# Maxima of half of the input taken from 16-bit absolute values that ScalarE makes, folded pairwise on VectorE

## The chip, the cores and the metric

The kernel runs on one core of a Trainium2 chip. The metric is the device time in microseconds (us) of one execution. The engines are called by their short names: PE (TensorE, the matrix engine), DVE (VectorE), ACT (ScalarE), POOL (GpSimd) and SP (SyncE, which here only issues DMAs).

## The reference, cut to what matters

The input u has 16 sequences of 512 tokens of width 256, in 32-bit floats. What is computed is one layer:

```
q, k, v = u Wq^T + bq, u Wk^T + bk, u Wv^T + bv       (per sequence, transposed to channels by tokens)
k       = causal_conv(k, k_kernel) + k_D * k           (by FFT in the reference)
kv      = k * v
y       = (causal_conv(kv, ssm_kernel) + D * kv) * q
x       = layernorm(u + y Wo^T + bo)
h       = relu(x W_fc^T)^2 ;  m = h W_proj^T
spikes  = 5 steps of a leaky threshold unit on m, mean of the spikes
out     = layernorm(x + spikes)
```

Nothing in the reference asks for a maximum. The kernel computes its products on PE with pairs of 16-bit floats (a high and a low part), and for that it scales each operand by a power of two, found from the operand's largest absolute value.

## The kernel before, in words

Every engine has its program written out by hand, in order, and the engines are held together by semaphores: `X.wait_ge(s, n)` holds engine X until semaphore s has reached n, `.then_inc(s, 1)` raises it when the instruction is done. There is no scheduler; on one engine the order of the text is the order of execution. `link(ins)` on DVE (semaphore `vlink`) makes the next DVE instruction wait for this one.

The span has a start-up, a first phase (projections and the two convolutions, 32 groups of 8 channels, up to some 390 us) and a second phase (output projection, layernorms, feed-forward and spikes, 16 sequences). The change lies in the start-up, which is as follows.

- SP issues the loads of the convolution kernels (`k_st`), the weights (`w_st`, `wn_st`) and then the transposed input `uT` in `NU` = 8 pieces of 1 MB (L308), each with a semaphore of its own, `ld_u[n]`. A piece is `u_st[:, :, n * UP:(n + 1) * UP]`, 128 partitions by 2 x 1024 elements; `u_st` is the tile `qy` under another shape.
- DVE takes maxima of the weights (L942, L945, into `part_max`); POOL spreads them over the partitions (`partition_all_reduce`, L582); DVE makes powers of two of them (`pow2`, L926 to L930) and releases ACT by `scales1` (a memset, L963).
- ACT then scales and splits the weights: `w_st` scaled (L427), its high part `w16[:, :, 0]` (L429, semaphore `w_hi`), the two convolution kernels scaled (L431) and their high parts (L435, `kpad_hi`). POOL makes the low parts: L585 for the weights (waits for `w_hi`, raises `w_lo`) and L588 twice for the convolution kernels (raises `kpad_lo`). ACT issues the DMA of the split weights to DRAM after `w_lo` (L438) and those of the split convolution kernels after `kpad_lo` (L443, `ksplit_out`). SP waits for these and copies the convolution kernels around in DRAM and back into SBUF as shifted windows (L316, L333), for which DVE waits at L1040.
- Meanwhile DVE takes the largest absolute value of every piece of u (L942 with the tile `u_maxima`, one reduction a piece), then of the eight results (L967, `u_maxima_done`). POOL spreads it over the partitions (L591, `u_max_done`), DVE makes the scale `d_scale` of it (L926 to L930, then a memset at L971 that raises `scale_u`).
- On `scale_u` ACT begins to turn u into its 16-bit high parts (L455), DVE follows with the low parts of six pieces (L986), POOL with those of the two pieces of `POOL_PIECES` (L608), and PE begins to project (L685).

POOL's instructions at this place stand in this order: L582 (all-reduce), L585, L588 twice, L591 (all-reduce), L608 twice.

`part(kb, ...)` cuts a tile out of one large SBUF tensor, `arena`, from the offset `at[0]` on; so most tiles carry the name `arena` in the profile.

Of the kernel before, what the change touches and what calls it, by code (L numbers as in the profile page):

```python
# [5 lines left out]
ALU = mybir.AluOpType  # L6
ACT = mybir.ActivationFunctionType
F32 = mybir.dt.float32
F16 = mybir.dt.float16
BF16 = mybir.dt.bfloat16  # L10
I32 = mybir.dt.int32
AX = mybir.AxisListType
# [4 lines left out]
DT = D // P  # L17
# [16 lines left out]
NU = 8  # L34
UP = TOK // NU
BOTH = 4
PIECES = 2
EPS = 1e-5
X1S = 2.0 ** 10
# [35 lines left out]
def build(nc, uT, u, wcat, wk_n, wv_n, bias, bo, k1, k2, kd1, kd2, woT, wfT, wpT, out):  # L75
# [11 lines left out]
    with ExitStack() as ctx:  # L87
        def sb(name, shape, dt):
            return ctx.enter_context(nc.sbuf_tensor(name, shape, dt))

        def sem(name):
            return ctx.enter_context(nc.semaphore(name))
# [7 lines left out]
        u_maxima = sb("u_maxima", [P, NU + 2], F32)  # L100
# [15 lines left out]
        KB = 256  # L116
        arena = sb("arena", [P, 628 * KB // 4], F32)
        at = [0]

        def part(kb, dt, pattern=None, **dims):  # L120

            a = arena[:, int(at[0]):int(at[0] + kb * KB)]
            at[0] += kb * KB
            if dt != F32:
                a = a.bitcast(dt)
            return a.rearrange(pattern, **dims) if pattern else a
# [28 lines left out]
        spread_max = part(0.5, F32)  # L155
        at[0] = 20 * KB
        stage_at = at[0]
        wf_st = part(8, F32, "p (t n) -> p t n", t=DT)
        wp_st = part(8, F32, "p (t n) -> p t n", t=FT)
        at[0] = stage_at  # L160
# [33 lines left out]
        ld_u = [sem(f"ld_u{n}") for n in range(NU)]  # L194
# [3 lines left out]
        u_maxima_done, u_max_done, scales1, scale_u, scales2 = (  # L198
            sem(n) for n in ("u_maxima_done", "u_max_done", "scales1", "scale_u", "scales2"))
        part_max2_done, turned2, spread2, all_max2_done, scales3 = (  # L200
            sem(n) for n in ("part_max2_done", "turned2", "spread2", "all_max2_done", "scales3"))
        sum_first, moments_first, wo_first = (sem(n) for n in ("sum_first", "moments_first", "wo_first"))
        vlink = sem("vlink")

        w_scaled, w_hi, w_lo, f_hi, f_lo = (sem(n) for n in ("w_scaled", "w_hi", "w_lo", "f_hi", "f_lo"))
        u_hi, u_lo, u_scaled, u_lo_pool = (sem(n) for n in ("u_hi", "u_lo", "u_scaled", "u_lo_pool"))
# [38 lines left out]
        u_st = qy[:, :].rearrange("p (t n) -> p t n", t=DT)  # L245
# [22 lines left out]
        def windows1_of(s, half):  # L268
            return T[:, s % 2 * 2 + half]
# [31 lines left out]
        def _(sp):  # L301
# [16 lines left out]
            def load_windows(conv, half, g):  # L318
# [4 lines left out]
                if conv == 0 and half == 0:  # L323
                    sp.wait_ge(kpad_out[g % NKP], 32 * (g // NKP + 1))
                run, c = row // PIECES, HG // PIECES
                if conv:
# [4 lines left out]
                else:  # L331
                    for n in range(PIECES):
                        sp.dma_start(windows1_of(g, half)[0:HP, n * c:(n + 1) * c].rearrange("p c a n -> p (c a n)"),  # L333
# [80 lines left out]
        def _(act):  # L414
# [5 lines left out]
            def as_pairs(dst, src):  # L420
                return dst.bitcast(F32), src.bitcast(F32)

            act.wait_ge(id_done, 2)
            nc.scalar.activation(*as_pairs(causal, step_st), ACT.Copy).then_inc(causal_done, 1)
            act.wait_ge(scales1, 1)

            nc.scalar.activation(w_st, w_st, ACT.Copy, scale=w_scale[:, cW:cW + 1]).then_inc(w_scaled, 1)  # L427
# [245 lines left out]
        def _(pe):  # L673
# [160 lines left out]
            def down_first(i):  # L834
# [6 lines left out]
                for f in range(FT):  # L841
                    pe.wait_ge(h_hi, i * FT + f + 1)
                    for t in range(DT if f < BOTH else 1):
                        for w in range(2):
# [12 lines left out]
            def down_second(part):  # L857
                for f in range(BOTH, FT) if part == 0 else range(FT):
                    for h, w in ((0, 0), (0, 1)) if part == 0 else ((1, 0),):
                        last = down_part(1, f, h, w, False, f == FT - 1 and h == 1)  # L860
                if part:
                    last.then_inc(down_done, 1)
# [52 lines left out]
        def _(dve):  # L915
            links = [0]

            def link(ins):

                links[0] += 1  # L920
                ins.then_inc(vlink, 1)
                dve.wait_ge(vlink, links[0])
# [18 lines left out]
            def max_abs(dst, src, axis=AX.XY):  # L941
                link(nc.vector.tensor_reduce(dst, src, axis, ALU.max, apply_absolute_value=True))  # L942
# [18 lines left out]
            dve.wait_ge(all_max_done, 1)  # L961
            pow2(w_scale[:, 0:3], w_unscale[:, 0:3], all_max[:, 0:3], scratch[:, 0:3])
            nc.vector.memset(part_max[:, cF:cF + 3], 0.0).then_inc(scales1, 1)  # L963
            for n in range(NU):
                dve.wait_ge(ld_u[n], 16)
                max_abs(u_maxima[:, n:n + 1], u_st[:, :, n * UP:(n + 1) * UP])
            nc.vector.tensor_reduce(u_maxima[:, NU:NU + 1], u_maxima[:, 0:NU], AX.X, ALU.max).then_inc(u_maxima_done, 1)  # L967
            dve.wait_ge(u_max_done, 1)
            pow2(d_scale[:, 0:1], d_unscale[:, 0:1], u_max[:, :], scratch[:, 0:1])

# [57 lines left out]
            def mask(conv, s, g, half):  # L1028

                if conv == 0:  # L1030
                    dve.wait_ge(t_in[s % 2 * 2 + half], 8 * PIECES * (g - s % 2) + 16 * PIECES)
                else:
# [286 lines left out]
```

## Time and profile before

| what | value |
|---|---|
| median of 3 runs | 845.57 us (838.6, 845.57, 846.23) |
| the profiled execution: time | 842.78 us |
| the profiled execution: span, first to last instruction | 841.1 us |
| outside the span in it | 1.7 us |
| mean granted TensorE clock | 0.981 of 2.4 GHz |
| busy over the span: PE, DVE, ACT, POOL | 88%, 84%, 63%, 46% |
| maxima of u on DVE (L942, tile u_maxima) | 8 reductions, 18.3 us busy |

A row of the profile names the line of the kernel, the engine, the operation and what it writes and reads; `128x2048 f32` is partitions by elements and type, `xN` a count. "Idle before" is how long the engine stood still ahead of it, and `<-` names what ended that: another engine's instruction, a DMA, or "issue", which is time in which the profile shows nothing that was waited for. `POOLq`, `ACTq` and `SPq` are the issuing sides of the engines: register work, configuration and DMA issue, which don't count as busy.

### The profile page before, as it was taken

The numbers are of one execution on the slowest core, as the hardware profiler recorded it, in microseconds if no ns is written. First come the engines' busy times: TensorE is split into PE (matmuls) and PEld (weight loads), VectorE is DVE, ScalarE is ACT, GpSimd is POOL, SyncE is SP. The second block draws the span as 40 slices with busy tenths as digits, with TensorE's granted clock in tenths as the row PEclk, the third lists the DMA queues.
The fourth block names the chain that finished last, engine by engine and source line by source line (L and its number), as shares of the span: only waits on it lengthen the run. The fifth ranks groups of instructions, "written<-read, shape, count | busy, mean of one in ns | idle before, by whom it ended". The sixth has DMA issues, their size and how long they took to land.

```text
span 841.1 us, 27057 instructions
## 1 busy us (share of the span) xinstructions
PE 740.2 (88%) x11447; PEld 540.4 (64%) x11447; DVE 710.5 (84%) x1204; ACT 530.6 (63%) x623; POOL 384.2 (46%) x302
## 2 busy tenths in 40 slices
PE   0087877999999999977999999999999999999993
PEld 0077877999999999965555555554555555555541
DVE  6898655787788778888878999999999999999896
ACT  1393656788887888775546665566655665556651
POOL 0332211222222322234457866687666866677622
PEclk9999999999999999989999999999999999999997
DMA  9995767999999997892100011101111011100001
GB/s 335 346 261 143 181 156 166 212 223 225 222 223 228 229 223 166 170 237 89 48 1 26 26 50 50 50 0 50 50 50 50 0 50 50 50 26 25 26 26 50
DMA packets 55369, 100.71 MB, mean 120 GB/s; under 512 B 5664, under 2 KB 41376, under 8 KB 53280
## 3 DMA queue, kind: packets, MB, share of 16 engines
q1 hardware_dynamic: 53952, 97.94, 45.4%
q10 hardware_dynamic: 1376, 2.23, 0.7%
q8 instruction: 25, 0.41, 0.2%
q14 instruction: 16, 0.13, 0.1%
HBM read 89.92 MB, written 27.01 MB: 139 GB/s over the span
## 4 chain that ended last, share of the span: by engine, by line
PE 43%; DVE 26%; POOL 17%; issue 9%; ACT 2%; DMA 2%; SPq 0%; POOLq 0%; DVEq 0%; ACTq 0%
PE ps L699 17%; POOL arena L632 15%; PE ps L685 14%; DVE arena L1222 8%; PE ps L832 5%; PE ps L825 4%; DVE u_maxima L942 2%; DVE arena L1170 2%; DVE arena L986 2%; DVE arena L1219 2%; DVE arena L1189 2%; DVE arena L1195 2%; PE ps L803 1%; POOL arena L639 1%; DMA arena<-in_wv_n 1%
## 5 line engine op out<-in xcount | busy, mean ns | idle before, releaser
L699 PE MATMUL ps<-arena 128*128 128x64 f16 (+3 forms) x6144 | 169.5, 181 | 18.2 <-issue 8.4
L632 POOL TENSOR_TENSOR arena<-arena 128x512 f16<-128x512 f32 x124 | 174.5, 1438 | 16.7 <-ACT arena L518 16.5
L699 PEld LDWEIGHTS ps<-arena 128*128 128x128 f16 x6144 | 166.7, 97 | 19.7 <-issue 15.5
L832 PE MATMUL ps<-arena 128*128 128x512 f16 x768 | 173.2, 379 | 3.0 <-POOL arena L632 3.0
L825 PE MATMUL ps<-arena 128*128 128x512 f16 x768 | 170.8, 379 | 2.5 <-DVE arena L1195 1.6
L685 PE MATMUL ps<-arena 128*128 128x96 f16 x3072 | 140.5, 209 | 16.8 <-issue 9.9
L596 POOL TENSOR_TENSOR arena<-arena 128x512 f16<-128x512 f32 x32 | 40.9, 1278 | 235.0 <-ACT arena L461 235.0
L685 PEld LDWEIGHTS ps<-arena 128*128 128x128 f16 x3072 | 135.5, 99 | 19.7 <-issue 12.1
L1211 DVE TENSOR_TENSOR arena<-arena 128x512 f32<-128x512 f32 x128 | 136.8, 1123 | 5.2 <-POOL arena L632 4.5
L514 ACT ACTIVATE arena<-ps,read_factor 128x512 f32<-128x512 f32 x128 | 87.9, 686 | 74.9 <-PE ps L825 57.9
L832 PEld LDWEIGHTS ps<-arena 128*128 128x128 f16 x768 | 73.9, 98 | 90.7 <-POOL arena L632 9.7
L825 PEld LDWEIGHTS ps<-arena 128*128 128x128 f16 x768 | 74.2, 98 | 88.8 <-issue 3.3
L471 ACT ACTIVATE arena<-arena 64x1792 f32<-64x1792 f32 x64 | 105.2, 1688 | 17.5 <-DVE arena L1058 17.5
L466 ACT ACTIVATE arena<-arena 64x1792 f32<-64x1792 f32 x60 | 98.7, 1688 | 2.4 <-DVE arena L1040 1.7
L518 ACT ACTIVATE arena<-arena 128x512 f16<-128x512 f32 x128 | 79.5, 624 | 32.5 <-DVE arena L1211 31.1
L1222 DVE SCALAR_TENSOR_TENSOR arena<-ps,stair_at,arena 128x512 bf16<-128x512 f32 x128 | 96.1, 751 | 4.5
L502 ACT ACTIVATE arena<-arena 128x256 f32<-128x256 f32 x126 | 65.3, 589 | 35.2 <-DVE arena L1181 34.7
L636 POOL TENSOR_TENSOR arena<-arena,eps 128x4 f32<-128x4 f32 x32 | 12.1, 377 | 143.6 <-DVE arena L1175 136.3
L1058 DVE COPY arena<-arena 32x3840 f16<-32x3840 f16 x64 | 72.0, 1162 | 1.0
L803 PE MATMUL ps<-arena 128*128 128x256 f32 x256 | 59.9, 388 | 2.9 <-ACT arena L495 2.9
L461 ACT ACTIVATE arena<-arena 128x512 f16<-128x512 f32 x32 | 20.2, 631 | 58.7 <-PE ps L699 49.9
L803 PEld LDWEIGHTS ps<-arena 128*128 128x128 f32 x256 | 49.6, 195 | 11.4 <-ACT arena L495 2.5
(114 smaller groups left out, 767.0 us busy)
## 6 DMA issues: line engine op xcount, KB each, us to landing
arena<-kpad_dram SPq DMA_DIRECT2D x192, 256.0 KB, 5.7
kpad_dram<-ksplit_dram SPq DMA_DIRECT2D x64, 256.0 KB, 5.9
qy<-in_uT SPq DMA_DIRECT2D x8, 1024.0 KB, 17.3
arena<-in_u SPq DMA_DIRECT2D x16, 512.0 KB, 4.1
out<-arena SPq DMA_DIRECT2D x16, 512.0 KB, 3.0
arena<-in_k SPq DMA_DIRECT2D x2, 512.0 KB, 5.1
ksplit_dram<-arena ACTq DMA_DIRECT2D x2, 512.0 KB, 4.1
arena<-in_wfT SPq DMA_DIRECT2D x1, 1024.0 KB, 9.2
```

The costliest lines, as they stand in the source:

```text
L466: nc.scalar.activation(*as_pairs(*shifted(windows1_of(s, half))), ACT.Copy).then_inc(c1_copied[half], 1)
L471: nc.scalar.activation(*as_pairs(*widened(windows2_of(g, half), HP)), ACT.Copy).then_inc(c2_copied, 1)
L514: nc.scalar.activation(relu_h[:, f], PH[:, f % 2], ACT.Relu, scale=read_factor[:, 4:5]).then_inc(relu_ready, 1)
L518: nc.scalar.activation(h16[:, 0, f], h_square[:, f % 4], ACT.Copy).then_inc(h_hi, 1)
L632: nc.gpsimd.tensor_tensor(h16[:, 1, f], h_square[:, f % 4], h16[:, 0, f], ALU.subtract).then_inc(h_lo, 1)
L685: last = nc.tensor.matmul(o, u16[:, x, t, tok:tok + P], wcur[:, w, t], start=(k == 0), stop=(k == 3 * DT - 1))
L699: last = nc.tensor.matmul(out[:, ch * COL + delta * B:(ch + 1) * COL], taps(c, tp)[:, delta * P:(delta + 1) * P], data[:, xp, ch * COL:ch ...
L803: last = nc.tensor.matmul(PW[:, j // 2, (j % 2) * D:(j % 2 + 1) * D], yT[:, t, j * P:(j + 1) * P], wo[:, t], start=(t == 0), stop=(t == DT ...
L825: last = nc.tensor.matmul(PH[:, f % 2], wf16[:, w, t, f * P:(f + 1) * P], x16[:, r, x, t], start=(k == 0), stop=(k == 3 * DT - 1))
L832: return nc.tensor.matmul(PD[:, t], wp16[:, w, f, t * P:(t + 1) * P], h16[:, h, f], start=first, stop=last)
L1211: nc.vector.tensor_tensor(h_square[:, f % 4], relu_h[:, f], relu_h[:, f], ALU.mult).then_inc(square_ready, 1)
L1222: ins = nc.vector.scalar_tensor_tensor(c, y, stair_at[:, n:n + 1], c, ALU.is_gt, ALU.add)
```

## The change

Four of the eight pieces of u (`CAST` = 4, the first four) get their maximum in another way. ACT turns each into 16-bit absolute values (bf16), in a new tile `u_abs` of 4 x 2048 elements; it does this ahead of its wait for `scales1`. DVE takes the larger of two pieces elementwise (`fold`), three times over 2048 elements, then over 1024 and 512, takes the maximum of the last 512 and raises it by 2^-8 of itself, since the rounding to bf16 can lower a value. The other four pieces are reduced as before. A copy puts the first result beside the other four for the last reduction.

```
@@ tiles and semaphore
+CAST = 4
+        at[0] = 32 * KB
+        u_abs = part(16, BF16, "p (n x) -> p n x", n=CAST)
+        at[0] = stage_at
+        u_cast = sem("u_cast")
@@ ACT
             act.wait_ge(id_done, 2)
             nc.scalar.activation(*as_pairs(causal, step_st), ACT.Copy).then_inc(causal_done, 1)
+            for n in range(CAST):
+                act.wait_ge(ld_u[n], 16)
+                nc.scalar.activation(u_abs[:, n].rearrange("p (t x) -> p t x", t=DT), u_st[:, :, n * UP:(n + 1) * UP],
+                                     ACT.Abs).then_inc(u_cast, 1)
             act.wait_ge(scales1, 1)
@@ DVE
             nc.vector.memset(part_max[:, cF:cF + 3], 0.0).then_inc(scales1, 1)
-            for n in range(NU):
+            def fold(dst, other):
+                link(nc.vector.tensor_tensor(dst, dst, other, ALU.max))
+
+            for n in range(0, CAST, 2):
+                dve.wait_ge(u_cast, n + 2)
+                fold(u_abs[:, n], u_abs[:, n + 1])
+            fold(u_abs[:, 0], u_abs[:, 2])
+            for size in (DT * UP // 2, DT * UP // 4):
+                fold(u_abs[:, 0, 0:size], u_abs[:, 0, size:2 * size])
+            link(nc.vector.tensor_reduce(u_maxima[:, 0:1], u_abs[:, 0, 0:DT * UP // 4], AX.X, ALU.max))
+            link(nc.vector.tensor_scalar(u_maxima[:, 0:1], u_maxima[:, 0:1], 1.0 + 2.0 ** -8, None, ALU.mult))
+            for n in range(CAST, NU):
                 dve.wait_ge(ld_u[n], 16)
                 max_abs(u_maxima[:, n:n + 1], u_st[:, :, n * UP:(n + 1) * UP])
-            nc.vector.tensor_reduce(u_maxima[:, NU:NU + 1], u_maxima[:, 0:NU], AX.X, ALU.max).then_inc(u_maxima_done, 1)
+            link(nc.vector.tensor_copy(u_maxima[:, CAST - 1:CAST], u_maxima[:, 0:1]))
+            nc.vector.tensor_reduce(u_maxima[:, NU:NU + 1], u_maxima[:, CAST - 1:NU], AX.X, ALU.max).then_inc(u_maxima_done, 1)
```

On ACT, from its first instruction to the high parts of the weights (L427 before, L436 after, is the scaling of `w_st`), before:

```order
L424 ACTIVATE arena<-arena 128x64 [waits id_done]
L427 ACTIVATE arena<-arena,w_scale 128x1536 [waits scales1]
L429 ACTIVATE arena<-arena 128x8x192 [waits w_scaled]
L431 ACTIVATE arena<-arena,w_scale 128x1024 x2
L435 ACTIVATE arena<-arena 128x2x512 [waits w_scaled] x2
```

And the same place after:

```order
L429 ACTIVATE arena<-arena 128x64 [waits id_done]
L432 ACTIVATE arena<-qy 128x2048 [waits ld_u0]
L432 ACTIVATE arena<-qy 128x2048 [waits ld_u1]
L432 ACTIVATE arena<-qy 128x2048 [waits ld_u2]
L432 ACTIVATE arena<-qy 128x2048 [waits ld_u3]
L436 ACTIVATE arena<-arena,w_scale 128x1536 [waits scales1]
L438 ACTIVATE arena<-arena 128x8x192 [waits w_scaled]
```

Four activations, each with a wait for a piece of u, now stand ahead of the scaling of the weights and of all that follows it on ACT.

On DVE, from the release of ACT to the end of the maxima, before (the eight reductions differ only in the piece that they wait for, `ld_u0` to `ld_u7`):

```order
L963 MEMSET part_max 128x3 [waits vlink]
L942 TENSOR_REDUCE u_maxima<-qy 128x1 [waits ld_u0]
...
L942 TENSOR_REDUCE u_maxima<-qy 128x1 [waits ld_u7,vlink]
L967 TENSOR_REDUCE u_maxima<-u_maxima 128x1 [waits vlink]
L926 TENSOR_SCALAR scratch<-u_max 128x1 [waits u_max_done]
```

And after:

```order
L974 TENSOR_TENSOR arena<-arena 128x2048 [waits u_cast]
L974 TENSOR_TENSOR arena<-arena 128x2048 [waits u_cast,vlink]
L974 TENSOR_TENSOR arena<-arena 128x2048 [waits vlink]
L974 TENSOR_TENSOR arena<-arena 128x1024 [waits vlink]
L974 TENSOR_TENSOR arena<-arena 128x512 [waits vlink]
L982 TENSOR_REDUCE u_maxima<-arena 128x1 [waits vlink]
L983 TENSOR_SCALAR u_maxima<-u_maxima 128x1 [waits vlink]
L951 TENSOR_REDUCE u_maxima<-qy 128x1 [waits ld_u4,vlink]
...
L987 COPY u_maxima<-u_maxima 128x1 [waits vlink]
L988 TENSOR_REDUCE u_maxima<-u_maxima 128x1 [waits vlink]
```

Four of the eight reductions are gone, seven instructions stand in their place, and the first two of these wait for ACT, not for a DMA.

On POOL the order is unchanged; before (`ISA` without a wait is what the trace names MODIFY_POOL_CONFIG at the same lines):

```order
L582 ISA all_max<-part_max 128x11 [waits part_max_done]
L585 ISA
L585 TENSOR_TENSOR arena<-arena 128x8x192 [waits w_hi]
L588 TENSOR_TENSOR arena<-arena 128x2x512 [waits kpad_hi] x2
L591 ISA
L591 ISA u_max<-u_maxima 128x1 [waits u_maxima_done]
```

Nothing moved there, and what each of the three kinds of instruction waits for is the same as before.

## Rows read from the trace of the kernel before

**Rows 1.** The chain that ended last, 36 to 43 us: start us, us, what.

```profile
34.48 2.30 DVE u_maxima L942
36.78 0.02 issue
36.80 0.17 DVE u_maxima L967
36.98 1.80 issue
38.78 0.39 POOL u_max L591
...
40.07 2.01 ACT arena L455
```

**Rows 2.** Timeline of POOL, 14 to 42 us: start us, us busy, instruction, [idle before].

```profile
16.96 0.43 POOL L582 PARTITION_ALL_REDUCE all_max<-part_max  x1 [14.31 <-DVE part_max L959]
24.60 3.09 POOL L585 TENSOR_TENSOR arena<-arena 128x1536 f16<-128x1536 f32 x1 [7.21 <-issue]
27.66 4.19 POOL L588 TENSOR_TENSOR arena<-arena 128x1024 f16<-128x1024 f32 x2
38.78 0.38 POOL L591 PARTITION_ALL_REDUCE u_max<-u_maxima  x1 [6.93 <-issue]
```

**Rows 3.** POOL's configuration instructions, by line: durations min/median/max ns, first and last start us.

```profile
L582 POOLq MODIFY_POOL_CONFIG  x2: 11/11/11, 2.6 to 2.6; - x2
L585 POOLq MODIFY_POOL_CONFIG  x2: 102/102/102, 17.3 to 17.4; - x2
L591 POOLq MODIFY_POOL_CONFIG  x2: 2/2/2, 32.0 to 32.1; - x2
L608 POOLq MODIFY_POOL_CONFIG  x2: 83/83/83, 39.1 to 39.1; - x2
```

**Rows 4.** Timeline of ACT, 2 to 60 us.

```profile
18.36 1.57 ACT L427 ACTIVATE arena<-arena,w_scale 128x1536 f32<-128x1536 f32 x1 [14.43 <-DVE part_max L963]
19.97 1.48 ACT L429 ACTIVATE arena<-arena 128x1536 f16<-128x1536 f32 x1
21.36 2.17 ACT L431 ACTIVATE arena<-arena,w_scale 128x1024 f32<-128x1024 f32 x2
23.44 1.99 ACT L435 ACTIVATE arena<-arena 128x1024 f16<-128x1024 f32 x2
27.71 0.35 ACTq L438 DMA_DIRECT2D w_dram<-arena  x1
31.88 0.91 ACTq L443 DMA_DIRECT2D ksplit_dram<-arena  x2
51.56 1.91 ACT L453 ACTIVATE arena<-qy 128x2048 f16<-128x2048 f32 x1
```

**Rows 5.** Line L308, the issues at 3.4, 5.9 and 14.0 us (pieces 0, 3, 7), one answer each.

```profile
L308 SPq DMA_DIRECT2D qy<-in_uT x1: 832/832/832, 3.4 to 3.4; - x1
DMA to landing us min/median/max: 11.2/11.2/11.2
...
L308 SPq DMA_DIRECT2D qy<-in_uT x1: 478/478/478, 5.9 to 5.9; - x1
DMA to landing us min/median/max: 16.3/16.3/16.3
...
L308 SPq DMA_DIRECT2D qy<-in_uT x1: 2439/2439/2439, 14.0 to 14.0; - x1
DMA to landing us min/median/max: 19.6/19.6/19.6
```

**Rows 6.** Timeline of all engines, 0 to 90 us: DVE's pieces of u, beside POOL and not.

```profile
42.21 4.62 DVE L986 SCALAR_TENSOR_TENSOR arena<-qy,d_scale,arena 128x2048 f16<-128x2048 f32 x2 [0.17 <-ACT arena L455]
55.52 4.29 DVE L986 SCALAR_TENSOR_TENSOR arena<-qy,d_scale,arena 128x2048 f16<-128x2048 f32 x1
59.28 4.48 POOL L608 TENSOR_TENSOR arena<-qy,arena 128x2048 f16<-128x2048 f32 x1 [1.62 <-ACT arena L453]
```

**Rows 7.** Groups by form on DVE: count, busy us, mean ns, idle before.

```profile
L942 DVE TENSOR_REDUCE u_maxima<-qy 128x1 f32<-128x2048 f32 x8 | 18.3, 2285 | 0.3
L945 DVE TENSOR_REDUCE scratch<-arena 128x2 f32<-128x512 f32 x2 | 1.4, 686 | 0.1
L942 DVE TENSOR_REDUCE part_max<-scratch 128x1 f32<-128x2 f32 x3 | 0.5, 155 | 0.1
```

**Rows 8.** Line L1040, 40 to 60 us: DVE's first 16-bit products, waiting for the windows.

```profile
L1040 DVE TENSOR_TENSOR arena<-arena x2: 410/410/411, 52.9 to 53.3; 64x512 f16<-64x512 f16 x2
```

**Rows 9.** Line L333, the issue at 42.7 us: the last half of the first windows.

```profile
L333 SPq DMA_DIRECT2D arena<-kpad_dram x1: 595/595/595, 42.7 to 42.7; - x1
DMA to landing us min/median/max: 8.3/8.3/8.3
```

## The prediction

> **What bounds the kernel now.** The change lies in the first 40 us, so I read only that stretch, and ask what sets the moment at which ACT may begin to turn u into 16-bit parts (`scale_u`, 40.07 us). Everything after it, 800 us, hangs on that moment and on the DMAs of the split convolution kernels, and the loops behind it have no tie to absolute time. A start-up that is d longer makes the kernel d longer.
>
> First view, the chain of waits [rows 1]. It walks back from ACT L455 at 40.07 through DVE's small scale steps to POOL's all-reduce L591 at 38.78, and then shows 1.80 us of "issue" before it reaches DVE's last reduction of u, whose result was there at 36.98. The chain goes on along DVE's eight reductions, and a hasty reader takes them as the bound. The 1.80 us is where to stop: DVE was done and POOL did not start.
>
> Second view, POOL's own timeline [rows 2]. POOL finished L588 at 31.85 (27.66 + 4.19) and sat idle 6.93 us until 38.78, with "issue" as its reason. The same had happened once before: L582 ended at 17.39, L585 began 7.21 us later at 24.60, though what it waits for, ACT's L429 (`w_hi`), was done at 21.45 (19.97 + 1.48) [rows 4]. The third view says what lies in both gaps: MODIFY_POOL_CONFIG runs right after the last instruction of the other kind, at 17.4 for L585 and at 32.0 for L591, when its semaphore wait has not even begun to matter [rows 3]. After a change of kind (all-reduce to elementwise and back) POOL's first instruction comes about 7 us after the configuration, whatever else is ready. At L582 and L608 the same 7 us lie in longer waits. In sentences the rest can do without: the Trainium skill, page GPSIMD Engine Reference (the part on wrapper-ucode dispatch), says that the first call into a freshly loaded kernel pays an instruction load of about 6 us; the trace agrees in kind, with 7.21 and 6.93. With 6 in place of 6.93 the two chains would still both wait for POOL, by 0.9 us instead of 1.8.
>
> So the path in this stretch is POOL's: load of code to 24.60, L585 3.09 us, L588 4.19 us, load of code 6.93 us, all-reduce at 38.78. Two other chains join it with slack: DVE's maxima (done 36.98, slack 1.80 us) and ACT's high parts of the weights (done 21.45, slack 24.60 - 21.45 = 3.15 us).
>
> **Part one: what ACT gains in work.** Four Abs activations over 128x2048, f32 in, 16 bit out. The nearest row is ACT L453, the same size and the same kind of types without a scale from a tile: 1.91 us [rows 4]. They wait for the pieces of u. Piece 0 lands at 3.4 + 11.2 = 14.6 us and piece 3 at 5.9 + 16.3 = 22.2 us [rows 5]; between pieces there are some 2.5 us, more than 1.91, so ACT keeps pace with the DMAs and the fourth Abs runs from 22.2 to about 24.15. That the copy at L424 and Abs share a table is likely, because the order of instructions after the change has one table load as before.
>
> ACT is in order. Behind these four stands `w_st`'s scaling, which began at 18.36 and now begins at about 24.2: 5.85 us later. That is the term with the price. Queued with it are `w_hi`, the convolution kernels' high parts, and ACT's two kinds of DMA issues. Who waits: POOL L585 waits for `w_hi`, which comes at 21.45 + 5.85 = 27.3 instead of 21.45. POOL is ready at 24.60, since its load of code started at 17.4 as before. It now starts at 27.35 or so: **2.75 us later**. Of the 5.85 us, 3.1 us vanish in the slack. The high parts of the convolution kernels are there in time for L588 (L435's first half ends near 24.5 + 5.85 = 30.35, POOL finishes L585 at 27.35 + 3.09 = 30.45; the second at 31.3, before 32.5). So POOL ends L588 at 34.6, configures, loads for 6.93 us, and the all-reduce starts at 41.55 rather than 38.78: + 2.77.
>
> The other branch is ACT's DMAs. The one at 27.71 goes to 30.5 and the ones at 31.88 to 34.65, both + 2.8, because they wait for POOL and not for ACT. The windows for DVE L1040 then come 2.8 us later, and so does DVE at L1040 [rows 8]. All chains are shifted alike, so no new wait arises between them.
>
> **Part two: what DVE loses and gains.** Four reductions at 2.29 us go: 9.1 us [rows 7]. In come three folds of 2048, one of 1024, one of 512, a reduction of 512 (0.69 us, the row of L945) and a scalar step and a copy at 0.16 (the row of a two-element reduction) [rows 7]. No row shows a 16-bit fold of this size. From below: L1040 takes 0.41 us for 512 16-bit elements [rows 8]; with 0.15 us of it fixed, as the two-element reduction shows, 2048 elements come to 0.15 + 4 x 0.26 = 1.2 us, 1024 to 0.67 us. From above: L986, two inputs from SBUF with 32-bit data, 2.31 us each when alone (4.62 for two) [rows 6]. I take 1.2, since L1040 is the same operation on 16-bit data. The Trainium skill, VectorE: DVE Perf Modes (the perf-mode tier table), has 1224 ns for a 16-bit two-input operation of 2048 elements and a single speed for reductions; by it the fold would cost the same as by my lower bound.
>
> But DVE cannot use this, because it waits for ACT. The first fold is hidden (pieces 0 and 1 are cast by 19.1, it runs to 20.4). The second waits for the fourth Abs, 24.15. From there: 1.2 + 1.2 + 0.67 + 0.41 + 0.69 + 0.16 and some 0.2 of gaps = 4.5, to 28.7. Four reductions at 2.32 including their gap bring it to 38.0, copy and last reduction to 38.35. Before it was 36.98. So DVE's maxima end 1.4 us **later** than before, not sooner. Even without that wait the gain would be small, since piece 7 lands only at 14.0 + 19.6 = 33.6 [rows 5]; its reduction cannot end before 35.9, and it ended at 36.78. Both are covered: POOL is not ready before 41.55, which leaves 3.2 us. With the dear folds (2.31) the maxima end near 41.4, still just covered.
>
> **The sum.** + 2.8 us from POOL's later start, nothing from DVE. Against the profiled execution: 842.78 + 2.8 = 845.6 (span 843.9). That execution lies 2.8 under the median shown; the three runs and it spread over 7.6 us. I set the prediction against the middle of all four executions, 844.2 (between 842.78 and 845.57): **847.0 us**, a loss of 0.33%. About 1% is what a measurement of this kernel can tell from no change, so this counts as no change.
>
> **Rivals.**
> 1. *POOL's gaps are not a load in the background, but a delay after the wait.* Then the 3.15 us before L585 and the 1.80 before L591 follow the release. Against it: two gaps of 7.21 and 6.93 that agree when measured from the configuration, and disagree when measured from the release [rows 1 to 4]. It would give L585 at 30.45, + 5.85; the all-reduce at 38.35 + 1.8 = 40.15, + 1.4; and the windows + 5.85. DVE reaches L1040 1.4 later (54.3) and waits for windows that come 5.85 later. L1040 had little slack (the last of its windows landed at 42.7 + 8.3 = 51.0 [rows 9]; now 56.9). Total about + 4: 848.2.
> 2. *Folds collide with POOL and DVE becomes the bound* (this one ends clearly slower than before). L986 takes 4.29 us beside POOL's L608 and 2.31 alone, while reductions take 2.29 beside POOL's L585 and L588 all the same; L608 itself took 4.48 [rows 2, 6, 7]. Two-input work on DVE collides, reductions do not. The Trainium skill, SBUF — State Buffer (the single rule), says the same. If folds are also dear (2.31 alone, 4.3 beside POOL), then from 27.35 on, when POOL works, the third fold, those of 1024 and 512 are slowed: third done at 30.2, then 2.2 and 1.2 us, and the rest ends at 34.6; four reductions 43.9, end 44.3. That is 2.7 us over 41.55, so + 5.5: 849.7. It decides from the point where folds cost over 2.3 us each. With 1.2 us folds, only the last small one meets POOL.
> 3. *Nothing or a small gain.* If the change doesn't hold ACT up, because the pieces land sooner or POOL's load is longer than I think, or if DVE's maxima are the bound after all as the chain suggests. Then the most is 0.9 us (to the landing of piece 7): 843.3 to 844.2. Against it: ACT's order and piece 3's landing at 22.2 are facts of the trace.
> 4. *Something outside this stretch*: DMA timing in the first phase that falls otherwise after a shift. No row speaks for it; either sign, a few us.
>
> **How the numbers follow.** Forecast 0.65; rival 1 0.10; rival 2 0.12; rival 3 0.08; rival 4 0.05. The range takes the spread of the runs shown with the forecast added (838.6 + 2.8 = 841.4 to 846.23 + 2.8 = 849.0), widened up to rival 2 (846.23 + 5.5 = 851.7, cut to 851) and down by one for rival 3: 840.5 to 851. All cases lie within 1% of before (8.4 us), so same 0.94, slower 0.05, faster 0.01.
>
> **What would show it in the profile after.** ACT: four rows of L432, about 1.9 us each, the last starting when piece 3 has landed (near 22.2), and L436 near 24.2. POOL: L594 (the low part of the weights) near 27.4, its idle time now ended by ACT and no longer by "issue"; the second load unchanged near 6.9 us; all-reduce near 41.6. DVE: folds at 1.2 us, a wait before the second fold, last maximum near 38.4, then some 3 us of waiting. ACT's first conversion of u near 42.8, against 40.07. I am wrong if POOL's first gap after `w_hi` stays at 3 us (rival 1), if a fold takes over 2 us or the all-reduce is released by DVE (rival 2), or if the first conversion is where it was and the time still moves.

## The result, and the profile after

The kernel after the change takes 847.19 us (median of 20 executions, 842.5 to 850.09), the kernel before 843.49 us (median of 20, 838.6 to 848.37). The ratio is 1.0042, with a 95% interval of 1.0026 to 1.0058: a loss of 2.2 to 4.9 us, under 1%. The profiled execution of the kernel after took 849.43 us (span 847.7 us).

The chain that ended last, 20 to 44 us of the kernel after (answers to [rows 1]); start us, us, what:

```profile
5.80 16.33 DMA qy<-in_uT
22.13 0.02 issue
22.15 1.92 ACT arena L432
...
24.16 1.24 DVE arena L974
25.42 1.24 DVE arena L974
26.68 0.70 DVE arena L974
27.41 3.21 DVE arena L974
30.65 0.70 DVE u_maxima L982
...
38.52 2.30 DVE u_maxima L951
...
41.03 0.17 DVE u_maxima L988
41.20 0.13 issue
41.32 0.39 POOL u_max L600
...
42.62 2.01 ACT arena L464
```

ACT's first conversion of u now starts at 42.62 us, against 40.07 [rows 1]: 2.55 later. The 1.80 us of "issue" ahead of POOL's all-reduce has shrunk to 0.13, an ordinary hand-over, and the chain goes on through DVE, the fourth Abs and piece 3's DMA. One row in it is out of line: the fold of 512 elements takes 3.21 us, where the fold of 1024 ahead of it took 0.70.

The timeline of POOL and ACT in the kernel after, 0 to 90 us (answers to [rows 2] and [rows 4]):

```profile
22.15 1.91 ACT L432 ACTIVATE arena<-qy 128x2048 bf16<-128x2048 f32 x1 [0.66 <-DMA qy<-in_uT]
23.97 1.56 ACT L436 ACTIVATE arena<-arena,w_scale 128x1536 f32<-128x1536 f32 x1
25.56 1.48 ACT L438 ACTIVATE arena<-arena 128x1536 f16<-128x1536 f32 x1
27.13 3.20 POOL L594 TENSOR_TENSOR arena<-arena 128x1536 f16<-128x1536 f32 x1 [9.85 <-ACT arena L438]
30.30 4.38 POOL L597 TENSOR_TENSOR arena<-arena 128x1024 f16<-128x1024 f32 x2
41.32 0.38 POOL L600 PARTITION_ALL_REDUCE u_max<-u_maxima  x1 [6.65 <-DVE u_maxima L988]
```

The scaling of the weights starts at 23.97 instead of 18.36, POOL's low part at 27.13 instead of 24.60, and its releaser is no longer "issue" but ACT. POOL is free at 34.68 (30.30 + 4.38), 2.83 later than before. What ends its second idle time is now put down to DVE. So two chains arrive at the all-reduce almost together, and the profile alone doesn't say which of them counts. "Load of code" is my name for what fills POOL's idle time after its configuration changes; the traces show the configuration and the wait behind it, and what POOL does in it no run shows.

### The profile page after: what moved, and what is told of

Same layout as the page of the kernel before. It is cut to its first block, busy times and chain, and to the rows that moved or that the text cites. A ratio compares the mean times of both kernels' runs of the same rounds, so it can differ in the third digit from the quotient of the medians.

```text
span 847.7 us, 27063 instructions
## 1 busy us (share of the span) xinstructions
PE 744.2 (88%) x11447; PEld 543.2 (64%) x11447; DVE 708.6 (84%) x1208; ACT 538.1 (63%) x627; POOL 385.0 (45%) x302
## 4 chain that ended last, share of the span: by engine, by line
PE 45%; DVE 24%; POOL 15%; issue 9%; DMA 4%; ACT 2%; SPq 1%; POOLq 0%; DVEq 0%; ACTq 0%
PE ps L708 17%; PE ps L694 14%; POOL arena L641 13%; DVE arena L1243 7%; PE ps L834 6%; PE ps L841 5%; DVE arena L1007 2%; DVE arena L1240 2%; DVE arena L1191 2%; DMA qy<-in_uT 2%; DVE arena L1216 2%; DMA arena<-kpad_dram 2%; DVE arena L1210 2%; PE ps L812 1%; DVE u_maxima L951 1%
## 5 line engine op out<-in xcount | busy, mean ns | idle before, releaser
L812 PE MATMUL ps<-arena 128*128 128x256 f32 x256 | 58.7, 382 | 2.9 <-ACT arena L504 2.9
L1061 DVE TENSOR_TENSOR arena<-arena 64x512 f16<-64x512 f16 (+1 forms) x128 | 45.5, 377 | 13.3 <-DMA arena<-kpad_dram 11.8
```

## The experiments

Besides the ratio I read two moments from each trace: when POOL's all-reduce of u starts, and when ACT's first conversion of u starts ("conversion" below). These come out alike to about 0.1 us in two profiles of one kernel, which the whole time does not: of the kernel before they are 38.78 and 38.69, 40.07 and 39.98, of the kernel after 41.32 twice, 42.62 and 42.61.

**Abs on ACT alone (e1).** ACT's four activations stay, DVE takes all eight maxima as before. `u_abs` is written and never read.

```
-            (folds, reduction and scaling of u_abs, 4 reductions, copy)
+            for n in range(NU):
+                dve.wait_ge(ld_u[n], 16)
+                max_abs(u_maxima[:, n:n + 1], u_st[:, :, n * UP:(n + 1) * UP])
```

> The changed kernel with its four Abs activations on ACT in place, ahead of the weights, but with DVE taking all eight maxima of u from the 32-bit pieces as before the change; the 16-bit tile is written and not read. My theory (ACT's delay of the weights makes POOL start late, and POOL's second load of code then sets the start): POOL's low part of the weights starts near 27.1 us instead of 24.6, DVE's maxima are done near 37.0, the all-reduce of u starts near 41.3 us all the same, idle time before it put down to issue, and the time is 1.003 of before. Rival (DVE's longer chain sets the start): with DVE's chain back at 37.0 the all-reduce starts at about 38.8 and the time is that of before.

Measured: 1.003 (1.0007 to 1.0052), 846.76 us. The timeline of this kernel:

```profile
27.03 3.10 POOL L594 TENSOR_TENSOR arena<-arena 128x1536 f16<-128x1536 f32 x1 [9.85 <-ACT arena L438]
30.10 4.21 POOL L597 TENSOR_TENSOR arena<-arena 128x1024 f16<-128x1024 f32 x2
36.59 0.16 DVE L976 TENSOR_REDUCE u_maxima<-u_maxima 128x1 f32<-128x8 f32 x1
40.59 0.38 POOL L600 PARTITION_ALL_REDUCE u_max<-u_maxima  x1 [6.29 <-issue]
41.88 7.68 ACT L464 ACTIVATE arena<-qy,d_scale 128x2048 f16<-128x2048 f32 x4 [10.97 <-DVE cell L980]
```

DVE is done at 36.75 and the all-reduce starts at 40.59 all the same. So the activations on ACT alone, with DVE as it was, make the conversion 1.8 us late (41.88 against 40.07) and the kernel slower. The rival, 38.8, is out. But it came 0.7 us short of my 41.3: the second load of code lasted 6.29 us here, not 6.93, and in the kernel after the all-reduce starts 0.73 later than this.

**The folds alone (e2).** No Abs on ACT; POOL fills `u_abs` with zeros at the very start, so that the maximum leaves out the first four pieces of u.

```
-            for n in range(CAST): (wait for ld_u[n], Abs on ACT)
+            nc.gpsimd.memset(u_abs.rearrange("p n x -> p (n x)").bitcast(F32), 0.0).then_inc(u_cast, CAST)
```

> DVE does the changed kernel's folds and its four remaining reductions, but ACT has no Abs: the 16-bit tile is filled with zeros by POOL at the very start, so the maximum leaves out the first four pieces of u. My theory: ACT's weights are back at 18.4 us and POOL at 24.6; DVE's folds all run before POOL works and take 1.22, 1.22, 1.22, 0.69 and 0.4 us, its maxima are done about 36.3 (piece 7 lands at 33.6), the all-reduce starts near 38.8 as before, held by POOL's load of code, and the time is that of before (1.000, within 0.002). Rival (DVE's chain sets the start): 0.7 us sooner than before. Second rival (folds themselves cost something elsewhere): slower than before with ACT and POOL unmoved.

Measured: 1.0011 (0.9989 to 1.0034), 844.02 us. DVE's maxima are done at 34.97, sooner than I reckoned (36.3), and the all-reduce waits for 3 us more:

```profile
24.68 3.08 POOL L591 TENSOR_TENSOR arena<-arena 128x1536 f16<-128x1536 f32 x1 [7.76 <-issue]
27.74 4.20 POOL L594 TENSOR_TENSOR arena<-arena 128x1024 f16<-128x1024 f32 x2
34.81 0.16 DVE L985 TENSOR_REDUCE u_maxima<-u_maxima 128x1 f32<-128x5 f32 x1
38.00 0.38 POOL L597 PARTITION_ALL_REDUCE u_max<-u_maxima  x1 [6.07 <-issue]
```

Making DVE's maxima 2 us shorter at no cost to ACT brings nothing that can be measured. The all-reduce is 0.7 to 0.8 sooner than before, which looks like the rival's number, but DVE had been done for 3 us; it is the load, 6.07 us after 31.94.

**One fold less (e3 and, once more, e10).** The changed kernel without the fold of 512; the reduction takes 1024 elements.

```
-            for size in (DT * UP // 2, DT * UP // 4):
+            for size in (DT * UP // 2,):
-            ... u_abs[:, 0, 0:DT * UP // 4], AX.X, ALU.max))
+            ... u_abs[:, 0, 0:DT * UP // 2], AX.X, ALU.max))
```

> The changed kernel without the fold of 512, which took 3.21 us beside POOL; the reduction after it takes 1024 elements instead of 512. My theory: DVE's maxima are done near 38.4 us instead of 41.2, and the all-reduce starts at 41.3 still, since POOL's load of code is done then; the time is as for the changed kernel, 1.003 to 1.004 of before. Rival (the collided fold is what sets the start at 41.3): the all-reduce starts when DVE is done or when a shorter load ends, below 41.0, and the time falls by the difference.

Measured: 1.0025 (1.0003 to 1.0047), 846.05 us.

```profile
27.04 3.21 POOL L594 TENSOR_TENSOR arena<-arena 128x1536 f16<-128x1536 f32 x1 [9.86 <-ACT arena L438]
27.32 1.22 DVE L982 TENSOR_REDUCE u_maxima<-arena 128x1 f32<-128x1024 bf16 x1
38.24 0.16 DVE L988 TENSOR_REDUCE u_maxima<-u_maxima 128x1 f32<-128x5 f32 x1
40.50 0.38 POOL L600 PARTITION_ALL_REDUCE u_max<-u_maxima  x1 [6.08 <-issue]
41.79 7.68 ACT L464 ACTIVATE arena<-qy,d_scale 128x2048 f16<-128x2048 f32 x4 [10.86 <-DVE cell L992]
```

The reduction in the fold's place starts beside the same POOL instruction, 0.28 us after it, and takes its full 1.22 us as if alone. DVE is done at 38.40, as my sum for DVE had it (38.35), and the all-reduce starts at 40.50. My theory, 41.3 still, is wrong here: without the fold of 512 the all-reduce starts 0.8 us sooner, when a shorter load ends, which is one of the rival's two ways. If the load is as short with the fold as without it, the blocked fold adds these 0.8 us in the kernel after; that condition is taken up under e9. The second profile repeats the moment:

> The changed kernel without the fold of 512 once more, one profile. My theory: DVE is done near 38.4 and the load of code starts the all-reduce, between 34.5 + 6.1 and 34.5 + 6.9 us, so 40.6 to 41.4; ACT's first conversion is 0.2 to 0.9 us sooner than in the changed kernel. Rival (the load always ends with DVE's chain): at 38.5.

It took 842.97 us once, without an interval. DVE was done at 38.38, the all-reduce started at 40.56 with 6.15 us of idle time before it, the conversion at 41.85.

**The kernel after once more (e9).**

> The changed kernel once more, one profile. POOL's second load of code took 6.93 and 6.65 us in the two profiles of the kernel before, 6.07 to 6.29 in the experiments. My theory now: POOL's low part starts near 27.1 again (2.4 later than before), and either the load or DVE's last maximum at 41.2, whichever is later, starts the all-reduce; with a load of 6.1 to 6.3 us it is DVE, and ACT's first conversion is near 42.5, 2.5 later than before. Rival (the first profile's hit of the fold by POOL was chance): the fold of 512 takes 0.4 us and the maxima are done at 38.4.

One time, 846.44 us. The fold was hit again (the last four folds take 6.45 us in both profiles), DVE was done at 41.09 and the all-reduce began at 41.32. That is 0.23 us after DVE, against 0.13 in the first profile. DVE's other hand-over to POOL in this trace, to the all-reduce at 16.74, took 0.14, so here a load of 6.74 us may have ended last and not DVE. What is shown is that the blocked fold makes DVE's chain 2.7 to 2.8 us longer (done at 41.19 and 41.09 with it, 38.40 and 38.38 without). That it makes the conversion 0.8 us later rests on a load of 6.1 to 6.3 us in the kernel after, as in e1, e3 and e10, and is likely but not shown.

**Two pieces instead of four (e4).**

```
-CAST = 4
+CAST = 2
-            fold(u_abs[:, 0], u_abs[:, 2])
```

> The changed kernel with two pieces in 16 bits instead of four (one fold of 2048, then 1024 and 512). My theory: ACT's second Abs ends at 19.0, the weights are 0.7 us late, which POOL's slack of 3.15 us covers; POOL starts at 24.6, the all-reduce at 38.8, the time is that of before (1.000, within 0.002). Rival (each piece cast costs its share, 0.6 us): the all-reduce at 40.0 and half the loss of the changed kernel. DVE's maxima are done near 36.6 and win nothing.

Measured: 0.9999 (0.9977 to 1.002), 843.13 us.

```profile
18.64 1.56 ACT L436 ACTIVATE arena<-arena,w_scale 128x1536 f32<-128x1536 f32 x1
25.15 3.09 POOL L594 TENSOR_TENSOR arena<-arena 128x1536 f16<-128x1536 f32 x1 [8.08 <-issue]
36.23 0.16 DVE L987 TENSOR_REDUCE u_maxima<-u_maxima 128x1 f32<-128x7 f32 x1
38.67 0.38 POOL L600 PARTITION_ALL_REDUCE u_max<-u_maxima  x1 [6.27 <-issue]
```

ACT's weights are late by a fraction of a us, POOL is released by "issue" again, the all-reduce starts where it did in the kernel before, and the loss is gone. The rival, 40.0 and half the loss, is out. The cost of Abs is not proportional to its work: it begins where ACT's delay exceeds POOL's slack.

**The kernel before, once more (e8).**

> The kernel before once more, unchanged, for how far profiles and times of one kernel differ: the length of POOL's two loads of code (7.21 and 6.93 in the first profile) and what lies behind the start-up. Both theories: ratio 1.000.

Measured: 0.9999 (0.9984 to 1.0014). POOL's two gaps were 7.68 and 6.65 us, against 7.21 and 6.93 [rows 2].

**Spreading the maximum by PE (e5, e6, e7).** The all-reduce of u is replaced by two transposes on PE with a reduction and a copy on DVE between them, in the kernel before (e5), in that of two pieces (e6) and in the kernel after (e7).

```
-            nc.gpsimd.partition_all_reduce(u_max[:, :], u_maxima[:, NU:NU + 1], ...)
+            nc.tensor.transpose(ps[0:1, 4, 0:P], u_maxima[:, NU:NU + 1], ident[:, :])         (PE)
+            link(nc.vector.tensor_reduce(scratch[0:1, 8:9], ps[0:1, 4, 0:P], AX.X, ALU.max))  (DVE)
+            nc.vector.tensor_copy(spread_max[0:1, :], scratch[0:1, 8:9].to_broadcast([1, P])) (DVE)
+            nc.tensor.transpose(ps[:, 5, 0:1], spread_max[0:1, :], ident[0:1, 0:1])           (PE)
+            link(nc.vector.tensor_copy(u_max[:, :], ps[:, 5, 0:1]))                           (DVE)
```

> The kernel before, with the maximum of u spread over the partitions by two transposes on PE (DVE reduces the turned row and copies it out) instead of by POOL's all-reduce; so POOL has no second load of code and no third one. My theory (POOL's load of code bounds the start of the kernel before): ACT's first conversion of u starts about 1.5 us after DVE's last maximum plus 0.9 for the scale, near 39.3 instead of 40.07, and 0.999 of before. Rival (the wait for L591 was no load but a plain cost of the hand-over): nothing is won, since two hand-overs to PE take its place.

Measured: 0.9997 (0.9975 to 1.002). The timeline of e5:

```profile
36.69 0.16 DVE L970 TENSOR_REDUCE u_maxima<-u_maxima 128x1 f32<-128x8 f32 x1
37.00 0.37 PE L710 MATMUL ps<-ident,u_maxima 128*1 128x128 f32 x1 [37.00 <-DVE u_maxima L970]
38.29 0.16 DVE L975 COPY u_max<-ps 128x1 f32<-128x1 f32 x1 [0.36 <-PE ps L712]
39.36 9.57 ACT L456 ACTIVATE arena<-qy,d_scale 128x2048 f16<-128x2048 f32 x5 [14.05 <-DVE cell L978]
```

The maximum is spread 1.6 us after DVE's last reduction (38.45 against 36.85), where POOL's way took 2.2 us (39.16 against 36.96) [rows 1]. The conversion moves from 40.07 to 39.36, as expected; 0.7 us is too little to show in the time.

> The same spreading by PE, and two pieces of u in 16 bits with folds. With POOL off the path DVE's maxima are the bound and are done 0.5 us sooner than with eight reductions, near 36.4. My theory: ACT's first conversion near 38.8, 1.3 us sooner than in the kernel before, 0.998 to 0.999 of before. Rival (cast pieces cost on ACT whatever is done with them): no sooner than with the spreading alone.

Measured: 0.9982 (0.9965 to 1.0). The conversion starts at 39.24, 0.8 us sooner than in the kernel before, not the 1.3 that I expected: DVE was done at 36.73, hardly sooner than in e5. The interval ends at 1.0, so this is at best a gain of a few tenths of a per cent, and I don't claim one.

> The changed kernel (four pieces) with the spreading by PE. POOL's code is off the path of the scale, so what is left is ACT's late fourth Abs and the fold of 512 that POOL blocks. My theory: DVE's maxima are done at 41.2 again, ACT's first conversion near 43.5, and 1.004 of before: as slow as the changed kernel or slower, though POOL's late start no longer counts for the scale.

Measured: 1.0082 (1.0059 to 1.0106), 850.82 us: the slowest kernel of the study. DVE's maxima are done at 41.18 as in the kernel after, and the conversion starts at 43.68, 0.2 later than expected. Against e5, which has the same spreading, the conversion is 4.3 us later (43.68 against 39.36), all of it from DVE's longer chain (41.18 against 36.85), the wait for the fourth Abs included. The spreading by PE is no gain here: in the kernel after POOL's maximum is out 0.5 us after DVE's last reduction (41.70 against 41.19), since the load was over by then, and the conversion there starts at 42.62.

The time says more than 4.3 us, 5 to 9. The trace has a second collision, between DVE's first 16-bit products and POOL's low part of u. First the rows of e7, then those of the kernel before:

```profile
56.97 4.64 DVE L1068 TENSOR_TENSOR arena<-arena 64x512 f16<-64x512 f16 x2
57.17 4.17 POOL L615 TENSOR_TENSOR arena<-qy,arena 128x2048 f16<-128x2048 f32 x1 [22.50 <-ACT arena L463]
76.28 0.26 DVE L1116 COPY arena<-arena 128x384 f16<-128x384 f16 x1 [2.49 <-issue]
```

```profile
52.93 0.74 DVE L1040 TENSOR_TENSOR arena<-arena 64x512 f16<-64x512 f16 x2
53.56 4.10 POOL L608 TENSOR_TENSOR arena<-qy,arena 128x2048 f16<-128x2048 f32 x1 [14.41 <-ACT arena L453]
70.32 0.26 DVE L1088 COPY arena<-arena 128x384 f16<-128x384 f16 x1 [2.49 <-issue]
```

Before the change DVE is 0.6 us ahead of POOL here and both products are through in 0.74 us. In e7 it is 0.2 us ahead, the second product begins just after POOL's instruction and takes 4.31 us, to 0.27 us after POOL's end. That costs 3.9 us, of which some come back behind it. At DVE's copy (the last row of each) e7 is 6.0 us behind the kernel before (76.28 against 70.32), which is inside the measured 5 to 9. This is read from one trace; no run takes the second collision away by itself.

## Why the prediction was right, point by point

**The sign, the size and the mechanism of POOL's late start held.** Predicted + 2.8 us, measured 2.2 to 4.9. Predicted 847.0 us, measured 847.19; that these two are so close is luck, since I set the kernel before at 844.2 and it measured 843.49, and the medians differ by 3.7. The Abs takes 1.91 us, the fourth starts at 22.15 (22.2 foreseen), the weights at 23.97 (24.2), POOL at 27.13 (27.35), the all-reduce at 41.32 (41.55), the conversion at 42.62 (42.8). That most of the cost comes because ACT is in order, and not through DVE's work, is shown by e1 (1.8 to 1.9 of the 2.6 us without any fold) and e4 (no cost when the delay is under the slack). With that rival 3, nothing or a small gain, is out as well.

**POOL's gaps run in the background, whether POOL has been released or not.** Rival 1 would have POOL start 3.1 us after `w_hi`. In the kernel after it starts 0.09 us after it (27.13 against 27.04), while the gap from the end of the first all-reduce has grown to 9.85 us. Rival 1 is out.

**The length of the load was mis-sized.** I took 6.93 us as fixed. Over the traces in which "issue" ends it, the load before the all-reduce lasted 6.07, 6.08, 6.15, 6.27, 6.29, 6.65 and 6.93 us, that before the low part of the weights 7.21 to 8.08. So "+ 2.77 from POOL" came out as 1.7 to 1.9 us in e1, e3 and e10 (conversion at 41.79 to 41.88 against 39.98 and 40.07). The short ones are not those of a late POOL alone (e2, 6.07, and e4, 6.27, had it free at 31.94 and 32.40). What sets the length is open.

**"Nothing from DVE" was wrong.** I let the fold of 512 meet POOL and take twice its 0.41 us at the worst. It took 3.21 us: it began at 27.41, 0.28 after POOL's L594, and ended at 30.62, just after POOL's 30.33. It didn't share, it waited out the whole POOL instruction. So DVE was done at 41.19 instead of 38.35 and its slack of 3.2 us was used up. The profile has DVE release the all-reduce, which I had put down as a sign of being wrong. The difference to e3 and e10 is 0.8 us (42.62 and 42.61 against 41.79 and 41.85); with the condition named under e9 that is the price of the blocked fold. Rival 2 named the mechanism and the wrong condition; it holds with folds of 1.22 us too. By this reading the blocked fold (+ 0.8) and the shorter load (- 0.9) nearly cancelled in my sum, which is why the total fitted better than its terms.

The price was misread from a row that I had. I took DVE's L986, 4.29 us beside POOL and 2.31 alone, as work at about half speed. It began at 55.52 and ended at 59.81 [rows 6]; POOL's instruction beside it, L608 at 53.56 (its row is shown under e7), ended at 57.66. So L986 stood for 2.14 us until POOL was through and then took 2.15. Read so, even a short fold that begins just behind a POOL instruction of 3.1 us should wait about 3 us.

**The fold's price** was 1.22 us for 2048 and 0.69 for 1024 elements, as taken (1.2 and 0.67).

**Between start-up and total.** The start-up accounts for 2.6 us, which lies inside the measured 2.2 to 4.9. The first two profiled spans differ by 6.6 us (847.7 against 841.1), the second pair by 0.0 (844.7 both), so single executions don't show a loss of this size. Much of their spread goes with TensorE's granted clock, 0.981 in the first profile of the kernel before against 0.972 of the kernel after, and 0.971 and 0.972 in the second pair. Over the 35 executions of the kernel before on record with e1 to e4 (their clocks lie between 0.965 and 0.984) a straight line gives 3.6 us more for 0.01 less clock; for the first pair that is an estimate of 3.3 us on top of the 2.6. That is something outside the stretch, as in rival 4, but it differs between executions of one kernel too. Whether the change costs anything behind the start-up no run shows.

## What to carry to other kernels

Read a wait put down to "issue" ahead of a POOL instruction together with POOL's configuration instructions: a change between kinds of POOL instruction may be a load of several us that starts when the last instruction ends, and then it, not the compute chain that the profile names next, is the bound. Before work is given to an idle engine, look at what stands behind it in that engine's order and at the slack of that work; the cost is zero up to the slack (e4), and beyond it POOL's start followed ACT's, while the conversion was later by less (1.8 to 1.9 us in e1 for a POOL that started 2.2 to 2.4 us later), because the load behind it came out shorter. Short two-input DVE instructions should not be placed beside long POOL instructions: the fold of 512 made the reduction after it shorter by 0.53 us (1.22 to 0.69) and took 3.2. Whether they meet can hang on 0.4 us of timing (e7), so look for such pairs a few us on either side of what the change moves.

## What the runs showed of the hardware that was not expected

A two-input 16-bit operation of DVE waited for the end of a POOL instruction that had begun 0.28 us before it (3.21 us for 512 elements), while a one-input reduction in the same place was not touched (1.22 us for 1024). POOL lost little there: its L594 took 3.20 and 3.21 us in the kernels with folds and 3.10 in e1, its two L597 4.38 us with the fold of 512 and 4.20 or 4.21 without. In e7 it was POOL's turn once: its second L615 took 6.83 us, where the second L608 of the kernel before took 4.48 [rows 6]. The Trainium skill, SBUF — State Buffer (the single rule), has this: `tensor_tensor` with both inputs in SBUF contends with GpSimd's reads, of the two that share the port pair one blocks fully for the whole instruction of the other, and on trn2 `tensor_reduce` never contends. The 3.21 and the 1.22 us above agree.

TensorE's granted clock steps down for some us at a time, and in other places from one execution to the next of the same kernel. Two profiles of the kernel after, first the one and then the other; the line is the same 96 matmuls:

```profile
81.86 5.85 PE L694 MATMUL ps<-arena 128*128 128x96 f16 x96 [1.95 <-DVE arena L1025]
```

```profile
81.84 4.25 PE L694 MATMUL ps<-arena 128*128 128x96 f16 x96 [1.95 <-DVE arena L1025]
```

The same two stretches by the view of windows, first and second profile, and below them the 16 matmuls of L812, where it is the second profile that is slower. The first number after the last bracket is the granted clock as a share of 2.4 GHz:

```profile
81.86:87.71 5.85, 5.85 (x96) 5.71 (x96) 0.71 0.79 195
81.84:86.09 4.25, 4.25 (x96) 4.10 (x96) 1.00 0.81 200
397.56:401.25 3.69, 3.69 (x16) 2.93 (x16) 1.00 0.00 0
394.24:399.62 5.38, 5.38 (x16) 4.11 (x16) 0.68 0.00 0
```

In the microsecond from 84 to 85 the first profile has a granted clock of 0.50, which is 1.2 GHz, and 16 matmuls; the second has 1.00 and 29. PE had been busy without a break since 81.86 when the clock fell, and stayed busy while it was low. What makes it fall in one execution and not in the next, no run here tells. It is one reason why a moment in the start-up repeats to 0.1 us and the time of the whole kernel only to some us.
